# An adaLN block with linear attention and routed experts: the last three groups routed in an order of their own

## The reference

```python
mod = silu(c) @ wmod                      # six rows per batch: sa, ca, ga, sb, cb, gb
ga, gb = sign(g) * max(|g|, 0.25)         # both gates
h = layernorm(x) * (1 + ca) + sa
x = x + ga * (linear_attention(h, w_qkv) @ w_out)   # 16 heads of 16, causal, phi = elu + 1
h = layernorm(x) * (1 + cb) + sb
# routed experts on h: logits = h @ w_router.T, softmax, top 2 of 8 experts,
# an expert takes the first 1280 tokens in order, weights renormalised over those kept
hidden = silu(h @ w_gate.T)               # one gate matrix for all experts
y = sum_e combine[:, e] * (hidden @ w_down[e].T)
out = x + gb * y
```

## Time and profile before

| | us |
|---|---|
| median of 3 runs | 872.08 |
| the three runs | 871.83, 872.08, 877.49 |
| the profiled execution | 877.7 |
| its span | 876.0 |
| busy in the span: TensorE | 790.7 (90%) |
| VectorE | 596.9 (68%) |
| ScalarE | 490.0 (56%) |
| GpSimd | 474.4 (54%) |
| TensorE's mean granted clock | 0.964 |

### The profile page before, as it was taken

One profiled execution on the slowest core, in us unless ns is written; L12 is line 12 of the kernel. 1 busy time (PEld: TensorE's weight loads), 2 busy tenths in 40 slices (PEclk: granted clock), 3 DMA queues, 4 the chain that ended last, 5 costly groups with the idle time before them and its releaser, 6 DMA issues.

```text
span 876.0 us, 24409 instructions
## 1 busy us (share of the span) xinstructions
PE 790.7 (90%) x9388; PEld 649.8 (74%) x9388; DVE 596.9 (68%) x1777; ACT 490.0 (56%) x1001; POOL 474.4 (54%) x591
## 2 busy tenths in 40 slices
PE   5899999999999999999999999622999998899993
PEld 4676776777777777777777776412999998899993
DVE  4666686887877887877877867660667746557652
ACT  5556666665765766756666664231655554454541
POOL 2202345664664764655666645574466656556654
PEclk9999999999999999999999999855999999999997
DMA  5579913323332333222222312224376665676553
GB/s 192 196 223 276 291 14 111 97 87 111 97 84 102 98 89 109 69 91 79 58 79 70 47 53 56 38 78 144 75 164 138 142 157 121 131 150 150 115 96 42
DMA packets 71427, 99.02 MB, mean 113 GB/s; under 512 B 7810, under 2 KB 52866, under 8 KB 71320
## 3 DMA queue, kind: packets, MB, share of 16 engines
q1 hardware_dynamic: 38744, 53.93, 22.6%
q0 software_dynamic: 21760, 31.66, 16.5%
q10 hardware_dynamic: 10816, 11.96, 4.3%
HBM read 46.84 MB, written 63.36 MB: 126 GB/s over the span
## 4 chain that ended last, share of the span: by engine, by line
PE 52%; DVE 13%; issue 12%; POOL 12%; DMA 6%; ACT 3%; POOLq 0%; ACTq 0%; SPq 0%; DVEq 0%
PE PJ L1325 9%; PE SCW L1229 6%; DVE Sm L891 6%; PE SCW L1265 6%; PE SCW L1477 5%; PE MD L1298 5%; POOL out L582 4%; DMA out<-EX,desti 3%; PE SCW L1249 3%; PE MD L1492 3%; PE SCW L1492 3%; PE SCW L1290 2%; PE PJ L1309 2%; PE SCW L1255 2%; PE MD L1239 2%
## 5 line engine op out<-in xcount | busy, mean ns | idle before, releaser
L483 POOL DMA_INDIRECT slot_rows<-Hrow,sloti x128 | 127.6, 997 | 150.9 <-PE SCW L1255 70.3
L891 DVE TENSOR_TENSOR Sm<-SCW,tri 128x1024 f32<-128x1024 f32 x128 | 150.6, 1218 | 57.2 <-PE SCW L1229 55.8
L582 POOL DMA_INDIRECT out<-EX,desti x80 | 127.3, 1592 | 30.3 <-issue 29.8
L1325 PE MATMUL PJ<-hT,w_qkv 128*128 128x512 f32 x384 | 108.5, 419 | 0.3 <-ACT hT L637 0.3
L1325 PEld LDWEIGHTS PJ<-hT,w_qkv 128*128 128x128 f32 x384 | 71.2, 192 | 20.5 <-issue 7.2
L1265 PE MATMUL SCW<-Sm,VA 128*17 128x128 f32 x2048 | 80.6, 275 | 0.0
L1229 PE MATMUL SCW<-QM,KT 32*128 32x256 f32 x1024 | 73.9, 402 | 7.1 <-ACT OTs L767 6.7
L1298 PE MATMUL MD<-w_og,ATs 128*128 128x256 f32 x256 | 73.3, 409 | 0.5 <-ACT ATs L756 0.5
L433 POOL TENSOR_TENSOR idle<-mhalf 128x1 f32<-128x1 f32 x100 | 27.1, 271 | 83.8 <-DVE EX L1164 57.3
L652 ACT ACTIVATE N<-X,nb,rs 128x256 f32<-128x256 f32 x128 | 66.3, 591 | 10.2 <-POOL nb L519 10.2
L648 ACT ACTIVATE EX<-PJ 128x512 f32<-128x512 f32 x64 | 37.9, 592 | 58.6 <-PE PJ L1325 58.6
(11 more groups left out here) (189 smaller groups left out, 1798.0 us busy)
## 6 DMA issues: line engine op xcount, KB each, us to landing
Hrow<-slot_rows SPq DMA_DIRECT2D x32, 516.0 KB
slot_rows<-erow ACTq DMA_DIRECT2D x1, 10400.0 KB, 45.7
X<-x SPq DMA_DIRECT2D x16, 512.0 KB, 4.7
out<-X SPq DMA_DIRECT2D x16, 512.0 KB
Hrow<-mod_rows SPq DMA_DIRECT2D x16, 512.0 KB, 8.1
QT<-slot_rows SPq DMA_DIRECT2D x8, 516.0 KB
slot_rows<-Hrow,sloti POOLq DMA_INDIRECT x128
N<-wd SPq DMA_DIRECT2D x4, 512.0 KB
```

Of the source, the lines that this page charges most:

```text
L483: pool.indirect_dma_start(xe, bass.IndirectOffsetOnAxis(sloti[:, 1 - gp, k, t:t + 1], 0), Hrow[:, 1 - gp, t, :], None, bounds_check=SLOTS ...
L582: pool.indirect_dma_start(out, bass.IndirectOffsetOnAxis(desti[s % 2][:, a:a + 1], 0), Ys[s % 2][:, a, :], None, bounds_check=TOK - 1, oob ...
L891: dve.tensor_tensor(o.rearrange("p c (k w) -> p c k w", k=2), SCW[:, 2 * pair:2 * pair + 2, :].rearrange("p k (c w) -> p c k w", c=DC), tr ...
L1325: last = mm(PJ[m % 2][:], w_qkv[:, wp, cc, m * P:(m + 1) * P], hT[:, hp, cc, :], start=(cc + i == 0), stop=(cc == DC - 1 and i == len(SPLI ...
```

## The change

A function routing(n) gives the group and the step of routing that slot n does. Up to slot 60 it is as before. From slot 61 on the steps are: group 13 "pick" (all thirteen steps of choose) in 61 and "place" in 62; group 14 "columns" in 63, "pick" in 64, "place" in 65; group 15 as before in 68 to 71. Group 14 is no longer modulated by GpSimd: TensorE transposes N2, ScalarE applies saca2 on the way to h2T, and VectorE makes the modulated rows at the end of slot 63. saca2 is made in slot 61, through PJ[0] instead of KR. In slot 63 TensorE's transposes of group 14 stand behind from_state, and ScalarE's columns behind ATs and ahead of OTs. In slot 64 VectorE makes its thirteen steps ahead of the last sum. GpSimd sends group 13 in slots 63 (three sends), 64 (three) and 65 (two). The diff, with renamed arguments and repeated conditions left out:

```diff
+        def routing(n):
+
+            late = {TILES - 3: "pick", TILES - 2: "place", TILES - 1: "columns", TILES: "pick", TILES + 1: "place"}
+            if n in late:
+                return (n + 1) // 4 - 2 if n != TILES + 1 else GROUPS - 2, late[n]
+            return n // 4 - 2, (("columns", "first", "second", "place")[n % 4] if n // 4 - 2 != GROUPS - 2 else None)
...
+                def departure(g):
+
+                    at_least(pool, rested, g)
+                    pool.wait_ge(gb_in[g % 2], 16 * (g // 2 + 1))
+                    pool.wait_ge(route, NR * g + NR)
+                    pool.wait_ge(numbered, g + 1)
+                    if g == GROUPS - 2:
+                        pool.wait_ge(h2_done, 4 * g + 4)
                     pool.tensor_tensor(idle[:, 5:6], mhalf[:, 0:1], mhalf[:, 0:1], ALU.add).then_inc(rested, 1)
...
+                if leaving and q == 0 and gn != GROUPS:
+                    departure(gn - 3)
...
-                if q == 3 and group_ok(gn - 1) and gn != GROUPS:
+                if q == 3 and group_ok(gn - 1) and gn < GROUPS - 1:
                     modulate()
...
+                if n == TILES - 1:
+                    departure(GROUPS - 3)
+                    send_row(0, 0)
+                    pool.wait_ge(knt_full, TILES)
+                    send_row(0, 1)
+                    pool.wait_ge(state_full, TILES)
+                    send_row(1, 0)
+                    pool.wait_ge(sent[0], 128 * (GROUPS // 2 - 1))
+                    number(GROUPS - 2)
                 if n == TILES:
-                    send_row(0, 0)
+                    pool.wait_ge(on_full, TILES)
+                    send_row(1, 1)
                     pool.wait_ge(at_full, TILES)
-                    send_row(0, 1)
+                    send_row(2, 0)
                     pool.wait_ge(op_full, TILES)
-                    send_row(1, 0)
+                    send_row(2, 1)
...
-                if q == 2 and group_ok(gn - 1) and gn != GROUPS:
+                if q == 2 and group_ok(gn - 1) and gn < GROUPS - 1:
                     modulate()
...
                 if n == TILES + 1:
-                    send_row(1, 1)
-                    send(2)
                     send(3)
...
+                def columns_out():
                     for cidx in range(DC):
-                        if gn == GROUPS + 1:
+                        if g >= GROUPS - 2:
...
+                if routed and step == "columns" and n != TILES - 1:
+                    columns_out()
...
                     act.activation(ATs[:].rearrange("p c i -> p (c i)"), MA[:, 0:D], ACT.Copy).then_inc(at_done, 1)
+                if n == TILES - 1:
+                    columns_out()
...
-                hold = [q == 1 and gn == GROUPS]
+                hold = [n in (TILES, TILES + 1)]
+                g, step = routing(n)
+                routed = group_ok(g)
...
+                    if routed:
+                        if step == "first" and k < 8 or step == "pick" and k < 13:
+                            choose(g, k)
...
                 between()
+                if n == TILES:
+                    hold[0] = False
+                    while small[0] < 13:
+                        between()
                 if tile_ok(n - 1):
...
-                if n == TILES + 1:
+                if n == TILES - 3:
 
                     dve.wait_ge(col2_full, 1)
...
+                if n == TILES - 1:
+
+                    dve.wait_ge(mb_in, 32)
+                    dve.wait_ge(n2_ready, 4 * (GROUPS - 1))
+                    dve.wait_ge(sent[0], 128 * (GROUPS // 2 - 1))
+                    for t in range(GT):
+                        dve.tensor_tensor(Hrow[:, 0, t, 0:D], N2[:, t, :], MB[:, BATCH - 1, 2, :],
+                                          ALU.mult).then_inc(h2_scaled, 1)
+                    for t in range(GT):
+                        dve.wait_ge(h2_scaled, 4 * (GROUPS - 2) + t + 1)
+                        dve.tensor_tensor(Hrow[:, 0, t, 0:D], Hrow[:, 0, t, 0:D], MB[:, BATCH - 1, 1, :],
+                                          ALU.add).then_inc(h2_done, 1)
...
+                if g == GROUPS - 2:
+                    pe.wait_ge(col2_done, 1)
                 for cc in range(DC):
                     for t in range(GT):
-                        row = N1[:, t, :] if gn == GROUPS + 1 else Hrow[:, hp, t, 0:D]
-                        last = pe.transpose(PJ[cc][:, t * P:(t + 1) * P], row[:, cc * P:(cc + 1) * P], ident[:])
+                        row = N1 if g == GROUPS - 1 else N2 if g == GROUPS - 2 else Hrow[:, g % 2]
+                        last = pe.transpose(PJ[cc][:, t * P:(t + 1) * P], row[:, t, cc * P:(cc + 1) * P], ident[:])
...
-                if n == TILES + 1:
+                if n == TILES - 3:
                     second_columns()
...
                     from_state(T, q, gp)
+                if n == TILES - 1:
+                    h2_transposes(g, gn)
...
-                if q == 0 and group_ok(gn - 2):
-                    logits(G, stage1)
+                if routed and step == "columns":
+                    logits(g, gn, stage1)
```

More of the change, by code:

```diff
@@ L708, in slot_ @@
                 stage1 = group_ok(nx)
-                if q == 1 and group_ok(gn - 2):
-                    act.wait_ge(lgt_full, G - 1)
+                g, step = routing(n)
+                routed = group_ok(g)
+                if routed and step in ("first", "pick"):
+                    act.wait_ge(lgt_full, g + 1)
                     act.activation(lgT[:], PJ[1][:, 0:P], ACT.Copy).then_inc(lgt_done, 1)
@@ L713, in slot_ @@
                     next_tile_queries(T, q, gp, tp, n)
[L714 to L717, removed]
-                if q == 0 and group_ok(gn - 2):
+                if routed and step in ("first", "pick"):
+                    take(lg, lg_ps[:, :, 0:E], lg_full, g)
+                if routed and step == "place":
+                    take(pos, pos_ps, pos_full, g)
+                def columns_out():
                     for cidx in range(DC):
-                        act.wait_ge(h2t_full, 2 * (G - 2) + cidx + 1)
-                        if gn >= 3:
-                            act.wait_ge(lg_full, G - 2)
-                        if gn == GROUPS + 1:
+                        act.wait_ge(h2t_full, 2 * g + cidx + 1)
+                        if g >= 1:
+                            act.wait_ge(lg_full, g)
+                        if g >= GROUPS - 2:
                             act.wait_ge(col2_done, 1)
@@ L778, in slot_ @@
                         stage1_v(G, 1, npar, nx)
-                if q == 2 and group_ok(gn - 2):
-                    g = G - 2
+                if routed and (step == "second" or step == "pick"):
                     act.wait_ge(route, NR * g + 8)
@@ L1009, in place @@
                 elif k == 4:
[L1010 to L1012 removed]
+                    if g >= 2:
+                        dve.wait_ge(sent[pg], 128 * (g // 2))
                     done(dve.tensor_copy(sloti[:, pg], slot[:]))
@@ L1056, in slot_ @@
                     masked_scores(T, 1, tp, n)
-                if q == 3 and group_ok(gn - 2):
-                    if gn == GROUPS + 1:
-                        dve.wait_ge(sent[gp], 128 * (GROUPS // 2 - 1))
+                if routed and step == "place":
+                    if g >= GROUPS - 3:
+                        dve.wait_ge(sent[g % 2], 128 * (g // 2))
                     if tile_ok(n - 1):
-                        normalise_heads(T, lambda: place_expert(gp), lambda: None)
+                        normalise_heads(T, lambda: place_expert(g % 2), lambda: None)
                     else:
-                        place_expert(gp)
+                        place_expert(g % 2)
                 elif tile_ok(n - 1):
@@ L1402, in slot_ @@
                 stage1 = group_ok(gn + 1)
+                g, step = routing(n)
+                routed = group_ok(g)
                 if tile_ok(n):
                     scores(T, q, gp, tp)
-                if q == 1 and group_ok(gn - 2):
-                    logit_rows(G)
-                if n == TILES + 1:
+                if routed and step in ("first", "pick"):
+                    logit_rows(g)
+                if n == TILES - 3:
                     second_columns()
-                if q == 0 and group_ok(gn - 2):
-                    h2_transposes(G, gn, gp)
+                if routed and step == "columns" and n != TILES - 1:
+                    h2_transposes(g, gn)
                 if stage1:
@@ L1417, in slot_ @@
                         stage1_v(G, 0)
-                if q == 3 and group_ok(gn - 2):
-                    positions(G, T, n)
+                if routed and step == "place":
+                    positions(g, gn)
                 if tile_ok(n - 1):
```

80 lines of the change are left out of this document (36 added, 44 removed).

## The result

The changed kernel took 870.93 us (median of 20 runs, 867.56 to 874.98), the kernel before 874.74 us (20 runs, 869.41 to 880.29). The ratio is 0.9956, with a 95% interval of 0.9939 to 0.9973: 3.8 us less by the medians, between 2.4 and 5.3 by the interval. I had said 3.25 less, and 868.8 us, counted from the first median of 872.08; from the 874.74 of this comparison the same 3.25 gives 871.5. The profiled execution took 871.01 us, with a span of 869.1; before 877.7 and 876.0.

The account below looks back on a forecast made before the run. A queue of 21 GpSimd sends was taken to bound the seam's tail. t0 (end of the last norm's nb) 0.75 us later, 4.0 gained behind it: -3.25, from 872.08 to 868.8 us; range 866.5 to 875.6.

Parts of the forecast that it names:

- rival (a): Behind t0 (end of the last norm's nb): group 15's route bounds, ScalarE's gap returns; -1.35 us, 870.7; chance 0.33.
- The sends moved up: GpSimd's queue behind t0: three sends of group 13 leave it, 3.84 us, with a longer send's 0.22 about 4.0.
- The route as the next bound: Group 15's route behind t0: gain 2.1 us if ScalarE's 2.9 us gap at lgT stays, 4.0 without it.
- The queue's own gap: GpSimd's 1.51 us idle, not 0.30, ahead of the send at 582.16; if gone too, gain 5.2 us.
- The modulation on VectorE: End of slot 63: eight products and sums, 2.79 us, put the last tile's normalising 1.0 us later; contention might add 1.9.
- Choosing and masks: VectorE, slots 61 to 64: masks of tile 62 0.86 us late, tile 63 1.2; thirteen steps fit ahead of the last sum.
- TensorE and ScalarE: Slots 61 and 63: OTs copy near 562.4, head rows end at 564.5 to 565.2, as late as before; VectorE later.
- The clock: TensorE's last output product may run at 2.4 GHz instead of 1.2, as idle time is filled: 0.25 us less.
- SyncE's columns: Gate columns of Hrow for group 15, one DMA landing near t0+12.7 under cover of the send queue: no cost.
- three signs of being wrong: nb later than 574.5, tile 63's head rows ending after 566, or expert phase over 2 us from 273.
- Rival (b): Slots 61 to 63: packed routing is exposed, t0 up to 5.6 us later; slower by +3.5, 875.6; chance 0.14.
- (c): Expert phase drowns the difference: median on the upper of two levels 5.5 us apart, 875.2 us; chance 0.07.

Follow-up runs that it names:

- the repeat: Changed kernel run and traced again without an edit: 872.07 us, 0.9992; in the passage on ScalarE's gap, the kernel before traced again.
- the paced one: Changed kernel with all eight sends of group 13 ahead of t0, meant in pairs released by TensorE steps: 869.61 us, 0.9941 of before.
- the one with both edits: Changed kernel with all eight group 13 sends paced ahead of t0 and VectorE's four modulation sums at the end of slot 65: 870.76 us, 0.9942.

## Why the prediction was right

**The number**: 870.93 us is 2.1 above the 868.8 of the forecast and next to the 870.7 of rival (a). That is the starting point, not the mechanism: 868.8 was counted from a median of three runs, and the twenty runs of the comparison put the kernel before 2.7 us higher. From 874.74 the forecast gives 871.5 and (a) 873.4, and the interval, 2.4 to 5.3 us less, leaves out (a)'s 1.35. Nor were there two levels 5.5 us apart: the twenty runs before spread over 869.4 to 880.3.

**The sends moved up**: right, and the whole of the gain. The queue alone was to bring group 15's first send to t0+15.5; it came at 15.65 and 15.62, and with the sends put back at 19.54.

**The route as the next bound**: right in its conclusion, wrong in its ground. Without ScalarE's gap the route was to be complete at t0+13.6; it was at 13.3 to 13.7, in time for the queue. But I took the gap for something that happened to one execution. It is in both traces of the kernel before (4.03 and 4.14 us of idle time ahead of lgT), and about half of it with the sends put back (2.70); in all traces with two sends or none of group 13 behind t0 the idle time is 1.20 to 1.43. ScalarE's timeline of the kernel before, repeated, and of the one with the sends put back:

```profile
580.72 0.28 ACT L711 ACTIVATE lgT<-PJ 128x128 f32<-128x128 f32 x1 [4.14 <-remote]
```

```profile
580.48 0.28 ACT L731 ACTIVATE lgT<-PJ 128x128 f32<-128x128 f32 x1 [2.70 <-remote]
```

So the change itself takes the gap away. Had it stayed, the sum for rival (a) gives 2.1 behind t0 instead of 3.9. That the forecast and not (a) came out is so in part luck. The queue's own gap, which I called odd too, is in every trace, at the same place in the program.

**The modulation on VectorE**: its price is right, its effect was partly covered. The eight took 2.77 us and stand directly ahead of den, one for one. den was to come 1.0 us later; counted from tile 61's masks it came 0.41 earlier in one trace and 0.45 later in the other. The contention with sends that the Trainium skill's page SBUF — State Buffer, section "Who interferes with whom", would allow did not appear on VectorE: 1.42 + 1.43 us beside a send, as without. The send that TensorE's head rows released beside them, at 561.98, took 1.66 us in place of 0.97, 1.47 in the repeat and 2.99 with the products made twice, and in all three it ended within 0.04 us of An on VectorE: what was held was the send, and it had time. Not every send is held: of the six in a row, two beside the same eight took 0.99 and 1.04.

**Choosing and masks**: 0.86 and 1.2 us late were the estimates for tiles 62 and 63. The repeat has 0.73 and 1.2, the first trace 0.48 and 0.34. The thirteen steps in slot 64 fit under the slow product, with 0.56 us of idle time left in the repeat. In the trace with the fast product they end last, at 566.39, 0.5 us behind it, so the last sum waits for them there.

**TensorE and ScalarE**: an error of nearly 2 us, though it changed nothing. Head rows were to be as late as ever; they ended 22.3 us behind tile 61's masks instead of 24.2. I had ScalarE's copy of OTs at 562.4; it began at 559.20, as the columns took 1.44 us and followed ATs at once. VectorE's eight were later anyway, and exchanging ScalarE's two steps moved nothing.

**The clock**: 0.25 us was the guess; the product ran at full clock for the most part in the first trace (1.34 us) and at half in the repeat (2.07). Between these two traces it decides some 0.6 us of t0.

**The sum**: t0 was to come 0.75 us later. It came 0.97 earlier in the first trace and 0.5 later in the repeat, so the term was too large by 0.2 to 1.7 us; the 4.0 behind t0 was 3.9 in both; and the seam is 4.9 or 3.4 us shorter where I had 3.25. **SyncE's columns** were issued 4.0 us behind t0 (4.1 was the estimate) and cost nothing. The spread of the times lies for the most part in the expert phase: "rest" runs from 270.5 to 276.2, and in the first pair of traces, 275.1 and 274.9, it is the same. None of the three signs of being wrong appeared. Rival (b) didn't happen, and (c) is no more than this spread.

**Two slips in the sum**, on which nothing turned: with the queue's own gap gone the first send would stand at t0+14.3, ahead of the t0+14.6 that the route allowed, so that gain ends at 5.0 and not 5.2; and 866.5 lies below what its terms give (868.8 - 1.2 - 0.4 = 867.2).

## What to carry to other kernels

Where a stage ends in a queue on one engine, count what stands in it behind the last thing that it waits for, and move entries, not work: three sends ahead of that point were the gain, and the earlier routing, which let them move, was worth nothing without them. After that, each next step gave less than its row said, because the same engine's gap or the next condition took it: work out what is late next for each us, up to the end. When one moves many small indirect DMAs, look at the trace of the other engines as well as at the sender's: the same eight sends cost nearly 8 us in one go at the start of slot 63, and nothing with the first two spread by TensorE's steps.

## What was not expected

**Eight sends in one go held up three other engines.** Eight in a row (1.28 us apart) from the start of slot 63 put TensorE, ScalarE and VectorE 8 us behind, with and without the 512 KB transfer beside it. It began early: ScalarE took up TensorE's transposes of An 4.1 and 5.5 us after they ended, during the third send, and TensorE's first gap falls into the fourth. The last hand-overs came 1.7 to 1.8 us after the last send had ended. The gap of ScalarE in the kernel before looks alike: there the run begins at t0+0.5, the hand-over from TensorE comes with the fifth send and is seen 1.1 us after the run's sixth, about when GpSimd has its own gap (in the repeat sends from 571.91 to 579.63, then none until 581.14; ScalarE goes on at 580.72). With two sends behind t0 that gap of GpSimd comes before the hand-over, and ScalarE waits no longer than usual.

But a row of sends is not the whole cause. Six in a row did no harm in the run made for it, nor in the paced one or the one with both edits, though hand-overs fell into the fourth to the sixth; nor did the seven that the changed kernel sends from 575.32 to 584.10, with hand-overs up to the fourth. So five traces show the stall or the gap, and others with as long a row don't; whether it hangs on the place in the program, on what the other engines have just issued, or on something else is open. No row shows what the engines wait for, and neither the eight at another place nor pauses of GpSimd's own between them were tried.

**Sends that move nothing cost the same.** In the us from 572.4 to 573.4 of the changed kernel the queue of these sends shows 80 packets and 0.00 MB (full rows would be 0.27 MB a send, 128 x 520 numbers). From the code I take it that rows beyond an expert's capacity fall out by their bounds. The sends take as long as full ones: 0.97 to 1.04 us each in the kernel before from 300 to 330 us, where seven of them moved about 0.28 MB each, and 0.97 us and 0.30 of issue here. So their pace looks like that of issuing on GpSimd, not of the transfer.
